# A two-layer convolution mixer with expert layers: 16 images in one sequence of stages, or two halves of 8 images in a pipeline of fixed slots

## What is computed

```python
x = x + L0_conv(_ln_c(x))              # mixer 0
t = t + L0_ffn(_ln_t(t))               # expert layer 0: token i goes to expert i % 4
x = x + L1_conv(_ln_c(x))              # mixer 1
t = t + L1_ffn(_ln_t(t))               # expert layer 1: a router picks 2 of 8 experts
# mixer, for each image:
p = x.reshape(B, C, 3, H // 3, 3, W // 3).mean(axis=(3, 5))   # 9 pooled tokens
t = layernorm(p @ pe_W + pe_b) * ln_g + ln_b
xc, z = split(t @ in_W)
u = silu(conv3(xc) + conv_b)           # over the 9 tokens, each channel by itself
dlt, Bp, Cp = split(u @ xproj_W)
delta = softplus(dlt @ dt_W + dt_b)
state = state + delta * (A * state + Bp * u)      # 9 steps, 16 states a channel
y = (sum(state * Cp) + u * D) * silu(z)
out = bilinear(y @ out_W)              # 9 tokens back to 24 x 12 pixels
# expert layer 0: inner width 512;  expert layer 1: inner width 256
h = silu(x @ gate) * (x @ up);  out = h @ down
```

## Time and profile before

| | us |
|---|---|
| median of 3 runs | 1349.18 (1343.6 to 1351.3) |
| the profiled execution | 1354.61 |
| its span, first to last instruction | 1352.8 |
| TensorE busy | 1097.6 (81%) |
| VectorE busy | 760.6 (56%) |
| ScalarE busy | 384.9 (28%) |
| GpSimd busy | 473.6 (35%) |
| mean granted TensorE clock | 0.870 |

### The profile page before, as it was taken

The page is one execution under the profiler, slowest core; times in us unless marked ns, Lnnn a source line. Parts: engine busy times, 40 slices in busy tenths (PEclk is TensorE's granted clock), DMA queues, the critical chain, the costliest instruction groups (busy, mean ns, idle before and its releaser), DMA issues.

```text
span 1352.8 us, 19414 instructions
## 1 busy us (share of the span) xinstructions
PE 1097.6 (81%) x6073; PEld 911.7 (67%) x6074; DVE 760.6 (56%) x1272; ACT 384.9 (28%) x771; POOL 473.6 (35%) x522
## 2 busy tenths in 40 slices
PE   7961783999897999999437862599999999999654
PEld 4541683999897999954335852487777777777432
DVE  6637597667768666586394868533333333333365
ACT  5414000111010111153321661133333333333232
POOL 0005524306107000167146623544444444443111
PEclk9966776999998999999567985599999999999755
DMA  9201111202103000097306864335553553532498
GB/s 346 55 28 43 50 45 50 71 17 73 47 17 102 17 11 15 2 315 261 136 0 189 312 255 155 123 134 203 185 196 122 202 196 105 202 106 81 153 388 336
DMA packets 59837, 180.85 MB, mean 134 GB/s; under 512 B 7117, under 2 KB 20021, under 8 KB 53253
## 3 DMA queue, kind: packets, MB, share of 16 engines
q0 software_dynamic: 25472, 101.73, 21.9%
q1 hardware_dynamic: 34324, 78.60, 16.3%
HBM read 115.22 MB, written 65.09 MB: 133 GB/s over the span
## 4 chain that ended last, share of the span: by engine, by line
PE 68%; DVE 19%; DMA 7%; ACT 4%; issue 2%; POOL 1%; DVEq 0%; SPq 0%; POOLq 0%; ACTq 0%
PE ps L604 7%; PE ps L606 7%; PE ps L605 7%; PE ps L484 6%; PE ps L703 6%; PE ps L704 6%; PE ps L705 6%; DMA sb_g<-y_dram 4%; DVE sb_hs L1047 4%; PE ps L721 3%; PE ps L723 3%; PE ps L722 3%; PE ps L505 3%; PE ps L686 3%; PE ps L571 2%; PE ps L652 2%
## 5 line engine op out<-in xcount | busy, mean ns | idle before, releaser
L604 PE MATMUL ps<-sb_xnH,sb_w 128*128 128x288 f32 x512 | 155.7, 304 | 32.0 <-DVE sb_xnL L1130 25.5
L605 PE MATMUL ps<-sb_xnH,sb_w 128*128 128x288 f32 x512 | 154.5, 302 | 0.0
L606 PE MATMUL ps<-sb_xnL,sb_w 128*128 128x288 f32 x512 | 154.1, 301 | 0.0
L703 PE MATMUL ps<-sb_w,sb_xtH 128*128 x320 | 141.0, 441 | 1.0 <-DVE sb_xtL L1299 0.4
L1299 DVE TENSOR_TENSOR sb_xtL<-ps,sb_xtH 128x512 fp32r<-128x512 f32 x80 | 55.3, 691 | 138.7 <-ACT sb_xtH L872 135.1
L453 POOL DMA_INDIRECT y_dram<-sb_ysb,sb_scatter_at x80 | 79.8, 997 | 151.4 <-ACT sb_ysb L890 140.7
L704 PE MATMUL ps<-sb_w,sb_xtL 128*128 x320 | 127.4, 398 | 0.0
L705 PE MATMUL ps<-sb_w,sb_xtH 128*128 x320 | 126.8, 396 | 0.0
L604 PEld LDWEIGHTS ps<-sb_xnH,sb_w 128*128 128x128 f32 x512 | 99.5, 194 | 33.3 <-issue 26.1
L834 ACT ACTIVATE sb_sg<-ps 128x288 f32<-128x288 f32 x64 | 26.3, 411 | 290.9 <-PE ps L606 288.1
L441 POOL DMA_INDIRECT sb_xs<-xn_dram,sb_gather_at x80 | 79.3, 991 | 63.5 <-POOL sb_gather_at L437 49.3
(11 more groups left out here) (217 smaller groups left out, 2702.3 us busy)
## 6 DMA issues: line engine op xcount, KB each, us to landing
sb_raw<-in_w_ffn POOLq DMA_DIRECT2D x48, 512.0 KB, 4.2
w_dram<-sb_pieces POOLq DMA_DIRECT2D x24, 1024.0 KB, 7.9
sb_w<-w_dram SPq DMA_DIRECT2D x24, 1024.0 KB
sb_g<-y_dram SPq DMA_DIRECT2D x36, 512.0 KB, 6.4
sb_X<-in_x SPq DMA_DIRECT2D x16, 576.0 KB, 9.1
xn_dram<-sb_XN SPq DMA_DIRECT2D x9, 1024.0 KB, 5.3
out_x<-sb_X POOLq DMA_DIRECT2D x16, 576.0 KB, 6.3
sb_Bb<-bc_dram SPq DMA_DIRECT2D x2, 2304.0 KB, 8.4
```

Source lines behind the costliest of these rows:

```text
L604: pe.matmul(out_ap, wh, xh, start=start, stop=False)
L605: pe.matmul(out_ap, wl, xh, start=False, stop=False)
L606: return pe.matmul(out_ap, wh, xl, start=False, stop=stop)
L703: pe.matmul(PS[:, 2 + s, :], xtH[:, s, k, :], wh, start=k == 0, stop=False)
```

## The change

The 16 images become two halves of 8. The first half's mixer 0 runs alone. Then expert layer 0 of half 0 runs in 96 slots (one slot is 12 matmuls of 288 columns), with mixer 0 of half 1 spread over the same slots; then expert layer 0 of half 1 with mixer 1, router and routing of half 0; then expert layer 1 of half 0 (43 row tiles, three slots each) with mixer 1, router and routing of half 1; then expert layer 1 of half 1 (43 tiles) with the combination of half 0; last the combination of half 1. Each engine has a generator `conv(l, h, at)` whose parts name their slot with `yield`; on every engine the expert work of a slot stands first and the mixer parts up to that slot after it. All loops are written out.

Other edits that go with it:
- patches take 18 tiles of 128 tokens a half (before 48 tiles of 96 in all); transposes use banks 4 and 5; the pooled sum bank 6;
- mixer parts use PSUM banks 4 to 7, expert layers banks 0 to 3. In layer 1 each tile has one PSUM buffer in place of two, and silu and product have one SBUF buffer;
- square roots on ScalarE are gone: GpSimd raises variances to the power -0.5;
- the sum over 16 states moves from TensorE to a reduction on VectorE; high and low part of the upsampled tokens are stacked on partitions, so one matmul does for two;
- expert layer 0 keeps no expert's weights: a ring of two blocks of 1024 columns is filled by ScalarE (high parts) and GpSimd (low parts), all weights once for each half, 48 blocks; the 24 pieces of layer 1 are split between them. SyncE issues the raw loads, in parts whose runs are 128 or 256 numbers;
- itH and xnH are cast on ScalarE, not on VectorE;
- layer 1's weights are fetched from w1_dram once for each half; their room in SBUF is the one that layer 0 used, so the first fetch and the first gathers wait for the end of layer 0;
- inW, outW, bc, Bb, rout, the stores of rows and images are issued by ScalarE.

The diff, cut to its core:

```diff
+TL = TILES // 2
+XR = 9
+LAG = 6
+FN = 288
+FC = HALF // E0 // FN
+PAIRS = KC * FC
+USES = 2 * KC * FC + KC * FC
+FFN = E0 * USES
+NM = 2 * TL + E1 - 1
+SIDE = 4
+class Beside:
+    def __init__(self, parts):
+        self.parts = parts
+        self.slot = next(parts, None)
+    def upto(self, slot):
+        while self.slot is not None and self.slot <= slot:
+            self.slot = next(self.parts, None)
+    def finish(self):
+        while self.slot is not None:
+            self.slot = next(self.parts, None)
+def split_schedule():
+    order = []
+    for n in range(2 * E0):
+        for i in range(PE1):
+            at = n * USES + 8 * i
+            order.append((at - 5, n * PE0 + 2 * i, None))
+            order.append((at - 1, n * PE0 + 2 * i + 1, None))
+            order.append((at + 1, None, n * PE1 + i))
+    return order
...
         def _(sp):
+            def raw_pieces():
+                for r, (slot, q, n) in enumerate(splits):
+                    yield slot
+                    sp.wait_ge(lo_done, r + 1)
+                    if n is not None:
+                        sp.dma_start(w1_dram[n], stage[:, :, :].bitcast(f32)).then_inc(w1_stored, 16)
+                    if r + 2 < len(splits):
+                        load_raw(r + 2)
...
+            sp.wait_ge(used, 2 * FFN)
+            sp.wait_ge(w1_stored, 16 * NP1)
+            for h in range(2):
+                for e in range(E1):
...
         def _(pool):
+                for j in range(JC):
+                    yield at + 41 + 2 * j
+                    if j == 0:
+                        pool.wait_ge(du_ready, c + 1)
+                        pool.wait_ge(bc_in, 16 * (c + 1))
+                    else:
+                        pool.wait_ge(scanned, c * JC + j)
+                    pool.tensor_tensor(db[:, :, :], du[:, j:j + 1, :].broadcast_to((P, NS, TT)), Bb[:, 0:NS, :],
+                                       ALU.mult).then_inc(db_ready, 1)
...
+            def low_parts():
+                for r, (slot, q, n) in enumerate(splits):
+                    yield slot
+                    pool.wait_ge(hi_done, r + 1)
+                    to = stage if q is None else ring[:, q % 2, :, :]
+                    pool.tensor_tensor(to[:, 1, :], raw[:, r % 2, :], to[:, 0, :].bitcast(f32), ALU.subtract)\
+                        .then_inc(lo_done, 1)
...
         def _(pe):
+            def gate_up(n, m, c, u):
+                q, pair = n * PE0 + m, n * PAIRS + FC * m + c
+                if c == 0 and u == 0:
+                    pe.wait_ge(lo_done, split_of[q] + 1)
...
+                if m:
+                    pe.wait_ge(mul_done if u else sg_ready, pair - FC + 1)
+                for k in range(KC):
+                    last = three(PS[:, 2 * c + u, 0:FN], weight(q, k, u), xnH[:, c, k, :], xnL[:, c, k, :],
+                                 k == 0, k == KC - 1)
+                last.then_inc(used, 1)
...
+            Beside(conv(0, 0, 0)).finish()
+            mix = [Beside(conv(0, 1, 0)), Beside(conv(1, 0, FFN + 1))]
+            for s in range(2 * FFN):
+                n, i = s // USES, s % USES
+                if i < 2 * PAIRS:
+                    gate_up(n, i // (2 * FC), i // 2 % FC, i % 2)
+                else:
+                    i -= 2 * PAIRS
+                    down(n, i // (2 * FC), i // 2 % FC, i % 2)
+                mix[s // FFN].upto(s)
+                if s % FFN == FFN - 1:
+                    mix[s // FFN].finish()
...
+            mix = [Beside(conv(1, 1, SIDE)), Beside(combine(0, SIDE))]
...
+            for i in range(2 * NM):
+                h, s = i // NM, 3 * (i % NM)
+                if i + 1 < 2 * NM:
+                    transposes(i + 1)
...
+                if i:
+                    pe.wait_ge(h_ready, i)
+                gate_up_rows(i, slot, (0, 1))
+                mix[h].upto(s)
+                if i:
+                    hidden_transposes(i - 1)
+                gate_up_rows(i, slot, (2, 3)).then_inc(g_up, 1)
+                mix[h].upto(s + 1)
+                if i:
+                    down_rows(i - 1, slot_of(i - 1)[1])
+                mix[h].upto(s + 2)
...
         def _(act):
+            for s in range(2 * FFN):
+                n, i = s // USES, s % USES
+                if i < 2 * PAIRS and i % 2 == 0:
+                    silu(n, i // 2)
+                if 2 <= i <= 2 * PAIRS and i % 2 == 0:
+                    hidden_high(n, i // 2 - 1)
...
+                high.upto(s)
+                mix[s // FFN].upto(s)
...
         def _(v):
+                for j in range(JC):
+                    yield at + 42 + 2 * j
...
+                    v.tensor_tensor_scan(flat(s), flat(s), flat(db[:, :, :]), 0.0, ALU.mult, ALU.add)\
+                        .then_inc(scanned, 1)
+                    v.wait_ge(scanned, c * JC + j + 1)
+                    link(v.tensor_tensor(s, s, Bb[:, NS:, :], ALU.mult))
+                    v.tensor_reduce(yy[:, j, :], s.rearrange("p n t -> p t n"), AX.X, ALU.add).then_inc(yr_ready, 1)
```

2082 lines of the change are left out of this document (1076 added, 1006 removed).

## The result

The changed kernel takes 1377.35 us (median of 4 runs, 1375.29 to 1379.38), the kernel before 1349.01 in the same runs: ratio 1.0216, 95% interval 1.0182 to 1.025. It is slower by 2.2%; the forecast was 1206 and the range ended at 1320. The profiled execution has a span of 1377.6 us.

A forecast was written before the change was run, and what follows sets the result against it. TensorE was busiest at 81%, but 617 us lay outside the expert layers, to hide under expert work. Stretches 136 + 223 + 257 + 13 + 306 + 231 + 44 made 1210 us of span, 1206 against the median; range 1110 to 1320.

The forecast's parts named there:

- First half alone: From load to first expert matmul: patches, mixer, upsampling, statistics and exchange of one half, 136 us.
- patch slots: Layer 0, slots 0 to 23 of a half, patches beside expert work: 62 us, set by TensorE.
- The chain slots 24 to 52: Layer 0, the mixer's chain beside expert work: lower bound 63 us, upper 102 if each hop stops TensorE, 72 taken.
- theory 4: Expectation for a follow-up run: 8 half-size expert preparations, 4 before, each stop TensorE; spreading them gains 20 to 40 us.
- The port: VectorE waiting on the port shared with GpSimd: 0.23 us for each of 14 exposed operations per expert, 0.13 per slot.
- The 20 to 30 us: Layer 0, both halves: extra cost over the sum if port locks last a whole instruction, as the skill says.
- The reduction taken by VectorE: Mixer's sum over states moved from TensorE: 0.6 to 2.6 us by half and full product, 1.3 taken.
- rival C: Waiting turns stop all behind them, nothing overlaps, mixers stand alone: 1369 us, slower than before; chance 0.08.
- Layer 1, half 0: 43 row tiles with mixer 1, router and routing of half 1 beside: 306 us, at least 271 by TensorE's work.
- Layer 1, half 1: 43 row tiles with the first half's combination: 215 + 8 of transposes + 8 of hops, 231 us.
- B: VectorE bounds both halves of layer 0 through locks and fixed turns, layer 1's chain at its upper bound: 1292 us; chance 0.22.
- the clock: Sign named for the forecast: TensorE's clock near 1.0 through both expert layers.

The follow-up runs named there:

- the version without low parts: The best version with GpSimd filling the weights' low parts with zeros instead of subtracting: 1257.47 us, ratio 0.9348 to the kernel before.
- the best version: Changed kernel with early row loads, scan turn split with air, expert preparation earlier, combination transposes and start later, smaller slot moves: 1298.79 us, ratio 0.9647.
- the serial run: Changed kernel with every mixer, routing and combination run alone, nothing beside the experts: 1525.58 us, ratio 1.1322 to the kernel before.
- the split scan: Changed kernel with scan, product and reduction in a slot each, later mixer parts three slots later: 1373.12 us, ratio 1.0176 to the kernel before.

## Why the prediction was wrong

Of the 171 us between 1206 and 1377, the order of the turns and the late row loads hold 77 (1.0216 to 0.9647, given back without a change of work), GpSimd's low parts some 40 more, most of it the lock if the changed kernel's 27 of 44 is a guide, and some 50 are left in the version without low parts (1257 against 1206), which no run settles.

- **First half alone**: 136 said, 141.3 measured. Right.
- **Slots**: the patch slots held: from the first expert matmul (141.3) to slot 24 (216.0) are 74.7 us in the first half and 65.5 in the second for my 62, most of the excess at the next expert's preparation.
- **The chain slots 24 to 52, "I take 72, nearer the low end because VectorE's load is the nearest row"**: this is the step that failed in layer 0. The windows of these slots, up to slot 53:

```profile
216.00:311.60 95.60, 65.15 (x412) 60.31 (x411) 63.31 (x75) 39.09 (x92) 39.46 (x16) 0.86 0.44 132
484.90:582.90 98.00, 68.58 (x423) 62.70 (x422) 65.02 (x77) 38.98 (x92) 44.84 (x16) 0.84 0.42 128
```

VectorE's load was nearly right (63 said, 63.3 and 65.0 busy), and it is two thirds of the time. The upper bound, 102, "if each hop stops TensorE's turn", was near the truth: 95.6 and 98.0. That is 50 of layer 0's 92 us. In the best version the chain ends five slots later, so I compare up to slot 58: the changed kernel takes 107.8 and 109.3 us, the best version 93.1 and 99.0, and my terms make 86 (72 and five of the eight upsampling slots). About half of what the stretch was over came back by moving turns and row loads alone; each of these stretches also holds one change of expert. A sum of an engine's work says what a stretch must take; with turns in a fixed order and two slots of buffer, the distance between a producer's turn and its consumer's decides.
- **Changes of expert**: my sum had no term for them. An expert alone is 10 us over its plain slots, and in the whole pipeline these changes fall on the scans. Of the other 42 us of layer 0 they are the likeliest part; the run that spread them out gave 7 us alone and 15 with the others. My theory 4 counted them wrongly as twice as many as before: the kernel before makes one preparation for each of its 16 chunks too. What differs in the code is the order: there VectorE scales and shifts behind the first and the second of a chunk's four products, here in slots 14 and 15, ahead of the last low part, for which TensorE stands 4.62 us in the serial run. A smaller part, 2.01 us there, may be that in the kernel before the down product had PSUM banks 4 to 7 to itself, which the mixer now holds, so that TensorE waits for VectorE's addition. No run took the two apart.
- **The port**: I took 0.13 us per slot, which enters the sum only where I let VectorE's load set the time: 101 slots of layer 0, 13 us, and 9 in the routing there. The lock costs at least 27 us and, with all that the low parts cost, at most 44. The Trainium skill (SBUF — State Buffer, section Who interferes with whom) says that the later one waits for a whole instruction, and this case's rows agree (the scan of 4.58 us above). The 20 to 30 us that I worked out from it as coming on top would make 42 to 52; what was measured lies between that and my 22, and does not tell which is nearer.
- **The reduction taken by VectorE**: 1.3 us said, 2.27 measured, inside my bounds of 0.6 to 2.6. With it the scan's turn on VectorE is 8.1 us in the stop shown, where rival C counted 3.8 for scan and product.
- **Layer 1, half 0**: 306 said, 329.2 measured. Three of its 43 tiles take 17.9 to 18.1 us from start to start, where a tile with nothing beside it takes 4.8; why was not looked into further.
- **Layer 1, half 1, which I "hold for firm"**: 231 said, 264.8 measured, a tile at 6.8 us beside the combination, over the 5.4 that I had named. The work was counted rightly (227.1 after two changes of slot); the wait between turns was not.
- **Rivals**: B named locks and turns, but on a VectorE that would be full, and gave 1292. C named the right mechanism, a late turn that stops TensorE's two slots of buffer; its price for a wholly serial kernel, 1369, was 157 too low, so "under about 13 hidden, the change is no gain" was wrong too: 149 us are hidden and it is still a loss. Of the 157, 84 are layer 0's experts (388 for 304), which had nothing for the changes of expert, 44 are mixer, router and routing of layer 1 (178.2 and 170.4 for 152 each), and 31 the combinations; the mixer of layer 0 was priced rightly (119.7 for 121), and the row tiles came out below their price. With its 1526 in place of 1369, the same hiding of 159 us as in my forecast would have given 1367, a loss, and its chance of 0.08 was far too low. That the measured 1377 lies 8 us from C's 1369 is luck: a price 157 too low and 149 hidden that C had at nothing cancel each other.
- **Signs**: the clock was to be near 1.0 through both layers and was 0.89 to 0.94; the gaps on TensorE released by VectorE in the chain slots spoke for C, as written, while VectorE's low parts of the hidden values, with a mean of 633 ns, spoke little for B.

## What to carry to other kernels

When two streams are woven into fixed slots, price each producer and consumer pair by the slots between them and by the longest turn that may stand ahead, not only each engine's load; two slots of air cost nothing and gave 29 us here. Judge a repair not only alone but also by taking it out of the best version: alone it may only move the stop to the next wait, as the split scan did (the stop behind it grew from 5.9 to 11.1 us). And price the serial form of the split kernel first, from rows of it if they can be had: here it takes 177 us more than the kernel before, most of it in the changes of expert and in the mixer and routing of layer 1, and overlap has to earn that back before it gains.

## What the runs showed of the hardware

A fill by GpSimd does not lock in these runs (the section of the Trainium skill named above says so too, of GpSimd instructions that only write): VectorE's subtraction of two SBUF operands had a mean of 633 ns beside GpSimd's subtractions and 458 beside three fills that kept GpSimd busy as long. A lock can last the whole instruction: the scan of 4.58 us beside a low part of 2.34, 2.56 when alone. 16 products with the identity, 128 x 72 fp32, took TensorE 5.7 us, against 2.27 for the reduction on VectorE. And a stop of TensorE is paid twice, once by standing and once by the matmuls behind it at the lower of its two levels, 0.24 us apart for 0.132: in the 20 row tiles above 11 of the 26.7 us that came back were busy time of TensorE.
